# A transformer decoder's second feed-forward: inputs turned one tile ahead, second quantiser passes on GpSimd, the last norm's statistics in the loop, output stored by tiles

## The reference

```
def _act_quant(x):                       # per token
    scale = 127.0 / clip(max(abs(x), axis=-1), 1e-05)
    return clip(round(x * scale), -128, 127) / scale
def _weight_quant(w):                    # ternary, one scale for the whole matrix
    scale = 1.0 / clip(mean(abs(w)), 1e-05)
    return clip(round(w * scale), -1, 1) / scale
def _bitlinear(x, w):
    return einsum('bsd,fd->bsf', _act_quant(x), _weight_quant(w))
h = silu(_bitlinear(x, W1))              # W1: 2048 x 512
x = layernorm(x + _bitlinear(h, W2))     # W2: 512 x 2048, layernorm over the 512 features
```

## Time and profile before

| | |
|---|---|
| median of 3 runs | 3617.8 us (3613.61, 3617.80, 3622.76) |
| profiled execution, own time | 3619.58 us |
| profiled execution, span from first to last instruction | 3617.7 us |
| mean granted TensorE clock | 0.948 of full speed |
| busy share of the span: PE, DVE, ACT, POOL | 87%, 71%, 59%, 41% |
| HBM traffic | 110.75 MB read, 4.54 MB written |

### The profile page before, as it was taken

One profiled execution on the slowest core, in us unless ns is written; L12 is line 12 of the kernel. 1 busy time (PEld: TensorE's weight loads), 2 busy tenths in 40 slices (PEclk: granted clock), 3 DMA queues, 4 the chain that ended last, 5 costly groups with the idle time before them and its releaser, 6 DMA issues. The chain is left out here.

```text
span 3617.7 us, 82755 instructions
## 1 busy us (share of the span) xinstructions
PE 3130.8 (87%) x29792; PEld 2190.2 (61%) x29792; DVE 2583.4 (71%) x4821; ACT 2125.8 (59%) x5429; POOL 1492.7 (41%) x1849
## 2 busy tenths in 40 slices
PE   6999788268999999999999999999999999984185
PEld 4666565245666666666767667666676666763042
DVE  3444389865777777777777777777777777776876
ACT  4444400146777766777667776677766777763453
POOL 1111277114554545545445455455554554530000
PEclk9999899678999999999999999999999999996698
DMA  4000011001111011010110101101011010001201
GB/s 186 13 13 1 8 44 41 18 25 46 31 25 31 23 39 32 25 31 19 42 32 23 32 19 42 32 19 37 19 42 32 19 37 19 32 18 47 93 1 47
DMA packets 43231, 120.72 MB, mean 33 GB/s; under 512 B 5825, under 2 KB 10049, under 8 KB 39489
## 3 DMA queue, kind: packets, MB, share of 16 engines
q1 hardware_dynamic: 42816, 115.30, 10.2%
HBM read 110.75 MB, written 4.54 MB: 32 GB/s over the span
## 5 line engine op out<-in xcount | busy, mean ns | idle before, releaser
L2000 DVE TENSOR_TENSOR delta_Pb<-delta_bank,delta_lev 128x512 f16<-128x512 f32 x448 | 311.0, 694 | 230.9 <-PE delta_bank L2326 230.9
L1578 POOL TENSOR_SCALAR_AFFINE_SELECT delta_LA<-delta_LA 128x512 f32<-128x512 f32 x128 | 81.6, 637 | 857.3 <-DVE delta_LA L2021 848.1
L1992 DVE SCALAR_TENSOR_TENSOR delta_F<-delta_bank,delta_cw,delta_F 128x510 f32<-128x510 f32 (+1 forms) x512 | 380.8, 744 | 67.6 <-ACT delta_far L1811 57.5
L2300 PE MATMUL delta_bank<-delta_xh,delta_qkvh 128*128 128x512 f16 x1024 | 391.4, 382 | 4.5 <-DVE delta_qkvl L1960 3.0
L2300 PE MATMUL delta_bank<-delta_xl,delta_qkvh 128*128 128x512 f16 x1024 | 391.4, 382 | 0.0
L2300 PE MATMUL delta_bank<-delta_xh,delta_qkvl 128*128 128x512 f16 x1024 | 390.1, 381 | 0.0
L1598 POOL TENSOR_TENSOR delta_F<-delta_F,delta_far 128x506 f32<-128x506 f32 x256 | 283.6, 1108 | 255.6 <-DVE delta_F L1992 255.6
L1805 ACT ACTIVATE delta_F<-delta_bank,delta_cw 128x512 f32<-128x512 f32 x256 | 178.9, 699 | 280.9 <-PE delta_bank L2300 279.6
L2009 DVE CAST delta_XT<-delta_bank 128x512 f16<-128x512 f32 x448 | 309.4, 691 | 44.4 <-PE delta_bank L2349 44.3
L1770 ACT ACTIVATE delta_Xi<-delta_bank 128x512 f16<-128x512 f32 x320 | 190.1, 594 | 180.4 <-PE delta_bank L2345 180.4
L2285 PE MATMUL delta_bank<-delta_zh,delta_xh 128*128 128x256 f16 x1024 | 279.4, 273 | 0.6 <-ACT delta_gz L1833 0.6
(11 more groups left out here) (350 smaller groups left out, 9247.1 us busy)
## 6 DMA issues: line engine op xcount, KB each, us to landing
delta_Gb<-g_rows SPq DMA_DIRECT2D x66, 512.0 KB, 5.4
delta_st_qkv<-in_Wqkv SPq DMA_DIRECT2D x17, 1024.0 KB, 8.4
conv_T<-filters SPq DMA_DIRECT2D x32, 256.0 KB, 3.1
delta_st_zo<-in_Wz SPq DMA_DIRECT2D x16, 512.0 KB, 8.9
delta_st_zo<-in_Wout SPq DMA_DIRECT2D x16, 512.0 KB, 6.2
ffn_ahead_W<-in_W SPq DMA_DIRECT2D x2, 4096.0 KB, 17.6
conv_ahead_C<-in_ctx_rev SPq DMA_DIRECT2D x1, 6144.0 KB, 27.7
attn_xt<-in_xT SPq DMA_DIRECT2D x8, 512.0 KB, 4.6
```

Source lines behind the costliest of these rows:

```text
L1992: ve.scalar_tensor_tensor(dst, src, cw_tap(i, 3 - lag), dst, ALU.mult, ALU.add)\
L2000: ve.tensor_tensor(left(Pb[:, lvl, :, :], lvl), comp(bank[5], lvl), bc(lev[:, lvl, :].rearrange("p (n s) -> p n s", s=1 << lvl), 1, 8), AL ...
L2300: ins = te.matmul(bk[:, :], ww[:, QKV[job], kc, :], xx[:, kc, tok:tok + 512], start=(m == 0), stop=(m == 11))
```

## The change

Five things:

1. **Input turned one tile ahead.** PE, ACT and DVE do their step for x(t+1) in iteration t: PE turns it behind up(t), ACT copies it behind Silu(t), DVE quantises it ahead of quantise_h(t-1). Tile 0 is done ahead of the loop.
2. **Second quantiser passes on POOL.** The subtraction and clipping into xq and hq (before: L1176, L1189) are issued on POOL, in the order x(0), x(1), h(0), x(2), h(1), and so on. DVE no longer waits for its own first pass; PE waits for POOL's signals.
3. **Statistics in the loop.** `moments` makes each tile's mean and variance on DVE behind its residual add (in the iteration after it, and for the last tile behind the loop), into a tile that outlives the stage.
4. **Last norm.** `last_norm_stage` has no statistics of its own. It scales five tiles on ACT, five on POOL and six on DVE.
5. **Output stored tile by tile.** SP issues 16 DMAs of 256 KB in the same stage, each when its tile is scaled, in the order of the three engines' first tiles, second tiles, and so on. The separate store stage with its barrier is gone.

```diff
--- before.py
+++ after.py
@@ -1022,7 +1022,7 @@
                 last.then_inc(tr.sem, 1)
 
 
-def ffn1_stage(nc, X, consts, ahead):
+def ffn1_stage(nc, X, consts, ahead, mv):
 
     with ExitStack() as ctx:
         pt = Parts(nc, "ffn1", ctx)
@@ -1042,11 +1042,12 @@
         xf, xq = sb("xf", [P, 2, D]), sb("xq", [P, 2, D], BF16)
         xqT = sb("xqT", [P, 2, KC, P], BF16)
         h = sb("h", [P, 2, FF])
+        st = sb("st", [P, 2, 6])
         hq = sb("hq", [P, 2, FF], BF16)
         hqT = sb("hqT", [P, 2, FC, P], BF16)
         g = {n: counter(n, c) for n, c in dict(
-            ib=1, mg=1, ps=1, pd=1, wsum=1, tot=1, wsc=2, w1=4, w2=4, w3=4, mx=1, inv=3, x1=2, xt=1, xc=1, m1=4, sl=4,
-            hx=1, hs=3, hq=2, ht=4, hc=4, m2=1, add=1).items()}
+            ib=1, mg=1, ps=1, pd=1, wsum=1, tot=1, wsc=2, w1=4, w2=4, w3=4, mx=1, inv=3, x1=1, x2=1, xt=1, xc=1, m1=4, sl=4, st=1, mo=1,
+            hx=1, hs=3, h1=1, hq=1, ht=4, hc=4, m2=1, add=1).items()}
         block = ctx.enter_context(nc.Block())
 
 
@@ -1064,6 +1065,26 @@
                 gp.partition_all_reduce(sc[:, 4 * m + 1:4 * m + 2], sc[:, 4 * m:4 * m + 1], P,
                                         bass.bass_isa.ReduceOp.add).then_inc(g["tot"].sem, 1)
 
+            def rounded_x(t):
+                pool.wait_ge(g["x1"].sem, g["x1"].at(1, t))
+                if t >= 2:
+                    pool.wait_ge(g["xt"].sem, g["xt"].at(1, t - 2))
+                gp.tensor_scalar(xq[:, t % 2, :], xf[:, t % 2, :], MAGIC, 127.0, ALU.subtract, ALU.min)\
+                    .then_inc(g["x2"].sem, 1)
+
+            def rounded_h(t):
+                pool.wait_ge(g["h1"].sem, g["h1"].at(1, t))
+                if t >= 2:
+                    pool.wait_ge(g["ht"].sem, g["ht"].at(4, t - 2))
+                gp.tensor_scalar(hq[:, t % 2, :], h[:, t % 2, :], MAGIC, 127.0, ALU.subtract, ALU.min)\
+                    .then_inc(g["hq"].sem, 1)
+
+            rounded_x(0)
+            for t in range(NT):
+                if t + 1 < NT:
+                    rounded_x(t + 1)
+                rounded_h(t)
+
         @block.scalar
         def _(act):
             s_ = nc.scalar
@@ -1094,7 +1115,7 @@
                 for n in range(NB):
                     act.wait_ge(g["m1"].sem, g["m1"].at(n + 1, t))
                     if t >= 2 and n == 0:
-                        act.wait_ge(g["hq"].sem, g["hq"].at(2, t - 2))
+                        act.wait_ge(g["hq"].sem, g["hq"].at(1, t - 2))
                     s_.activation(h[:, t % 2, n * 512:(n + 1) * 512], bank[n][:, :], ACT.Silu,
                                   scale=tok[:, 0, t:t + 1]).then_inc(g["sl"].sem, 1)
 
@@ -1105,10 +1126,12 @@
                 s_.activation(xqT[:, t % 2, :, :].rearrange("p a b -> p (a b)"),
                               bank[4][:, 0:256].bitcast(BF16), ACT.Copy).then_inc(g["xc"].sem, 1)
 
+            xcopy(0)
             for t in range(NT + 1):
                 if t < NT:
-                    xcopy(t)
                     up(t)
+                if t + 1 < NT:
+                    xcopy(t + 1)
 
                 j = t - 1
                 if j >= 0:
@@ -1168,12 +1191,9 @@
                 dve.wait_ge(g["mx"].sem, g["mx"].at(1, t))
                 scales(0, t, None, 0, g["inv"])
                 xx = xf[:, t % 2, :]
-                ve.tensor_scalar(xx, X[:, t, :], inv[:, 0, t:t + 1], MAGIC, ALU.mult, ALU.add)\
-                    .then_inc(g["x1"].sem, 1)
-                dve.wait_ge(g["x1"].sem, g["x1"].at(1, t))
                 if t >= 2:
-                    dve.wait_ge(g["xt"].sem, g["xt"].at(1, t - 2))
-                ve.tensor_scalar(xq[:, t % 2, :], xx, MAGIC, 127.0, ALU.subtract, ALU.min).then_inc(g["x1"].sem, 1)
+                    dve.wait_ge(g["x2"].sem, g["x2"].at(1, t - 2))
+                ve.tensor_scalar(xx, X[:, t, :], inv[:, 0, t:t + 1], MAGIC, ALU.mult, ALU.add).then_inc(g["x1"].sem, 1)
 
             def quantise_h(t):
                 dve.wait_ge(g["sl"].sem, g["sl"].at(4, t))
@@ -1182,40 +1202,49 @@
                     .then_inc(g["hx"].sem, 1)
                 dve.wait_ge(g["hx"].sem, g["hx"].at(1, t))
                 scales(1, t, None, 1, g["hs"])
-                ve.tensor_scalar(hh, hh, inv[:, 1, t:t + 1], MAGIC, ALU.mult, ALU.add).then_inc(g["hq"].sem, 1)
-                dve.wait_ge(g["hq"].sem, g["hq"].at(1, t))
-                if t >= 2:
-                    dve.wait_ge(g["ht"].sem, g["ht"].at(4, t - 2))
-                ve.tensor_scalar(hq[:, t % 2, :], hh, MAGIC, 127.0, ALU.subtract, ALU.min).then_inc(g["hq"].sem, 1)
-
+                ve.tensor_scalar(hh, hh, inv[:, 1, t:t + 1], MAGIC, ALU.mult, ALU.add).then_inc(g["h1"].sem, 1)
+
+            def moments(t):
+                dve.wait_ge(g["add"].sem, g["add"].at(1, t))
+                ve.bn_stats(st[:, t % 2, :], X[:, t, :]).then_inc(g["st"].sem, 1)
+                dve.wait_ge(g["st"].sem, g["st"].at(1, t))
+                ve.bn_aggr(mv[:, t, :], st[:, t % 2, :]).then_inc(g["mo"].sem, 1)
+
+            quantise_x(0)
             for t in range(NT + 2):
-                if t < NT:
-                    quantise_x(t)
                 if t == 0:
                     weight_scale(1)
                     clipped(1)
+                if t + 1 < NT:
+                    quantise_x(t + 1)
                 if 0 <= t - 1 < NT:
                     quantise_h(t - 1)
                 j = t - 2
+                if j >= 1:
+                    moments(j - 1)
                 if j >= 0:
                     dve.wait_ge(g["m2"].sem, g["m2"].at(1, j))
                     ve.scalar_tensor_tensor(X[:, j, :], bank[7][:, :], tok[:, 1, j:j + 1], X[:, j, :], ALU.mult,
                                             ALU.add).then_inc(g["add"].sem, 1)
+            moments(NT - 1)
 
         @block.tensor
         def _(pe):
             te = nc.tensor
             pe.wait_ge(g["ib"].sem, g["ib"].at(1))
+
+            def turned_x(t):
+                pe.wait_ge(g["x2"].sem, g["x2"].at(1, t))
+                if t >= 1:
+                    pe.wait_ge(g["xc"].sem, g["xc"].at(1, t - 1))
+                for kc in range(KC):
+                    last = te.transpose(bank[4][:, kc * 64:(kc + 1) * 64].bitcast(BF16),
+                                        xq[:, t % 2, kc * P:(kc + 1) * P], ib[:, :])
+                last.then_inc(g["xt"].sem, 1)
+
+            turned_x(0)
             pe.wait_ge(g["w3"].sem, g["w3"].at(4))
             for t in range(NT + 2):
-                if t < NT:
-                    pe.wait_ge(g["x1"].sem, g["x1"].at(2, t))
-                    if t >= 1:
-                        pe.wait_ge(g["xc"].sem, g["xc"].at(1, t - 1))
-                    for kc in range(KC):
-                        last = te.transpose(bank[4][:, kc * 64:(kc + 1) * 64].bitcast(BF16),
-                                            xq[:, t % 2, kc * P:(kc + 1) * P], ib[:, :])
-                    last.then_inc(g["xt"].sem, 1)
                 if t < NT:
                     pe.wait_ge(g["xc"].sem, g["xc"].at(1, t))
                     for n in range(NB):
@@ -1225,9 +1254,11 @@
                             last = te.matmul(bank[n][:, :], xqT[:, t % 2, kc, :], w1q[:, kc, n * 512:(n + 1) * 512],
                                              start=(kc == 0), stop=(kc == KC - 1))
                         last.then_inc(g["m1"].sem, 1)
+                if t + 1 < NT:
+                    turned_x(t + 1)
                 j = t - 1
                 if 0 <= j < NT:
-                    pe.wait_ge(g["hq"].sem, g["hq"].at(2, j))
+                    pe.wait_ge(g["hq"].sem, g["hq"].at(1, j))
                     for n in range(4):
                         if n >= 2:
                             pe.wait_ge(g["hc"].sem, g["hc"].at(n - 1, j))
@@ -2529,15 +2560,63 @@
             turns(nc, ENG.PE, turn)
 
 
-def store_stage(nc, X, out):
+THIRDS = (range(0, 5), range(5, 10), range(10, NT))
+
+
+def last_norm_stage(nc, X, mv, out):
+
     with ExitStack() as ctx:
-        stored = Parts(nc, "store", ctx).counter("done", 0, 16)
+        pt = Parts(nc, "last", ctx)
+        var, rs, t, nb = (pt.sb(n, [P, NT]) for n in ("var", "rs", "t", "nb"))
+        variance, tab, newton, shift = (pt.counter(n) for n in ("var", "tab", "newton", "shift"))
+        by_act, by_pool, by_dve = (pt.counter(n) for n in ("by_act", "by_pool", "by_dve"))
+        stored = pt.counter("stored", 0, 16)
         block = ctx.enter_context(nc.Block())
 
         @block.sync
         def _(sp):
-            sp.dma_start(out.rearrange("b (h p) d -> p (b h) d", p=P), X[:, :, :]).then_inc(stored.sem, 16)
-            sp.wait_ge(stored.sem, stored.at(1))
+            for n in range(6):
+                for tiles, done in zip(THIRDS, (by_act, by_pool, by_dve)):
+                    if n < len(tiles):
+                        sp.wait_ge(done.sem, done.at(n + 1))
+                        sp.dma_start(out[:, tiles[n], :], X[:, tiles[n], :]).then_inc(stored.sem, 16)
```

(44 more changed lines are left out.)

## The result

The changed kernel is slower: 3647.45 us at the median (3642.7 to 3652.05, 4 runs) against 3620.09 for the kernel before (3613.61 to 3622.76, 4 runs), a ratio of 1.0078 [1.0056, 1.0101]. The forecast was 3599, faster. What happened is rival 3: POOL is so slow at these passes that its chain bounds the loop.

What follows compares the result with a forecast made beforehand. PE was taken to bound the feed-forward loop, with holes, and the end to be serial. The terms +0.9 - 7.15 + 0.85 + 0.87 - 9.65 - 4.9 sum to -19.1 us, giving 3599 us, chance 0.62; range 3592 to 3608.

Steps and rivals of the forecast that it cites:

- rival 3: Feed-forward loop: POOL so slow that its chain bounds the loop and more than eats the end's gain; 3633 us, chance 0.04.
- Period, 7.2 + S/2 from S = 4.8: Feed-forward loop: with S = H + Xp, POOL's two passes, its two-tile chain sets the period per tile from S = 4.8 us.
- 9.60 with POOL hidden: Steady feed-forward loop: POOL's passes are hidden and the period per tile is 9.60 us, 0.55 less than before.
- The slipped copies: ACT's queue: the input copy ahead of the four hidden copies moves the first from 4.25 to 4.78 us; without slipping, period 9.07.
- Start of the loop, +0.9: Tile 2's input waits behind hidden tile 0 on POOL, so its up-projection starts at 3438.0 instead of 3437.07, costing 0.9 us.
- PE's clock: Granted clock at the 1.2 GHz level in tile 2, behind the longer wait at the start, was named as a wrong sign.
- Ahead of the loop, 0: From the feed-forward stage's start to the first up-projection: a change of 0 us.
- Last tile, +0.85: End of the loop: POOL's 2.0 us plus 0.05 hand-over replaces DVE's 1.23, making the last tile 0.85 us later.
- The statistics' +0.87: After the last residual add: the last tile's statistics, 0.68 + 0.15 and a hand-over, cost 0.87 us.
- DVE and POOL "mostly miss each other": Feed-forward loop: DVE and POOL passes sharing a port lock mostly do not overlap, so the forecast loses nothing.
- rival 2: POOL at a two-input pace, H = 3.75 and Xp = 1.1: 3606 us with DVE's input pass caught, upper bound 3618; chance 0.14.
- Last norm, -9.65 and store, -4.9: Kernel's end: statistics leaving the last norm gain 9.65 us; the first store issued earlier, by tiles, gains 4.9 us.

Runs made afterwards that it cites:

- kernel 7: kernel 4 with 44 unused matmuls in odd tiles ahead of PE's wait for POOL; 1.0065 against the kernel before, 3639.29 us.
- run 1: The changed kernel with both second quantiser passes back on DVE; 0.9944 against the kernel before, 3595.16 us.
- run 3: The changed kernel with only the input's second pass on POOL, the hidden tile's back on DVE; 0.9928 against the kernel before, 3589.23 us.
- run 9: The changed kernel with POOL's two tensor-scalars replaced by casts, the clip at 127 left out; 0.9944 against the kernel before, 3596.37 us.
- run 10: The changed kernel with only the input's pass on POOL, hidden copies ahead of the input copy, last norm on ACT and DVE; 0.9903 against the kernel before, 3581.09 us.
- run 6: The kernel before with only the new end: statistics in the loop, last norm on three engines, stores by tile; 0.9953, 3599.88 us.
- run 8: The kernel before plus a POOL memset and one-column tensor-scalar beside its store; 0.998, 3608.84 us.
- kernel 4: The changed kernel with DVE's first input pass on ACT, both second passes still on POOL; 1.0079 against the kernel before, 3644.68 us.
- run 2: The changed kernel with only the hidden tile's second pass on POOL, the input's back on DVE; 1.0043 against the kernel before, 3632.89 us.
- run 5: The kernel before with only the two second quantiser passes on POOL, old order and old end; 1.0081, 3645.75 us.

## Why the prediction was wrong

**The step that failed** is the size of two terms: "I take H = 2.0 us for the hidden tile and Xp = 0.65 us for the input tile, and keep 1.9 and 5.3 as bounds of H." H is 7.08 and Xp 1.97. The price was read from the row with the same kinds of operands, the cast, and the upper bound from a row with two tensors. Neither holds the new operation's arithmetic, and the bound was no bound: the tensor-scalar costs more than both. The prediction knew that POOL's pace was the open question, and that the sum is zero near H = 5.2 and +11 near 3 ns a column; it gave this 0.04, because "No row of POOL is that slow". A row that is not there was taken for evidence against.

Step by step:

- *Period, 7.2 + S/2 from S = 4.8:* right in its mechanism. With S = 9.05 it gives 11.73; kernel 7, which takes the clock away, measures 12.19, of which 0.43 is POOL's slowed input pass.
- *9.60 with POOL hidden:* right, 9.54 (runs 1, 3, 9). The slipped copies were the reason that it was not less: run 10 puts them first and gets 9.06, the prediction's 9.07.
- *Start of the loop, +0.9:* the same two prices make it +7.3, measured +9.2. 1.8 of the rest is PE's clock behind the wait of 9.23 us (7.58 - 5.76). The prediction had named this clock as a sign of being wrong, but had no term for it. In runs 1 and 9, without the slow passes, it was +1.3 and +1.8; but runs 6 and 8, whose loop is the old one, have 12.9 and 12.8 there too, so a term of 0.9 is below what these executions resolve.
- *Ahead of the loop, 0:* wrong. The first input's pass was moved to POOL, and the prediction did not follow it past the all-reduce in POOL's queue, nor knew of the idle time behind it: +2.4.
- *Last tile, +0.85:* +5.95 by H, and 1.95 on top because PE, after 6.48 us idle, did a part of the tile at the 1.2 GHz level. The statistics' +0.87 was right.
- *DVE and POOL "mostly miss each other":* the text said that with a slower POOL they meet, and they do (4.11 us for L1196). It had 3 us for that in rival 2; kernel 7 shows some 5 for its kind of meeting. The changed kernel's 13 periods exceed the formula by 8.9 us, and its own trace divides them. Followed back from tile 15 by its waits for POOL, the path is six chains over two tiles and one plain tile of 9.54 us. In three of the chains POOL gets the hidden tile late, at 10.48, 10.28 and 9.49 us in place of 8.56, because DVE's stretched input pass holds up the maximum: 4.6 us in all. In four the link from the turning to L1254 is slow, 8.45, 7.44, 6.87 and 6.55 us in place of 5.76, with the granted clock at 0.50 in it: 6.3. The plain tile takes 2.2 off, and small hand-overs are the rest.
- *PE's clock:* named only for tile 2, with no term in the sum. It cost 1.8 us there, 6.3 in the 13 periods and 2.0 in the last tile, the largest single part of what the right prices leave open. Filling the wait in kernel 7 gave 8.5 us of the stretch against kernel 4.
- *Last norm, -9.65 and store, -4.9:* right to a hundredth, as far as the first store. That "the three engines make one in 0.8 to 1.2 us" was wrong by the same price: a tile takes POOL 2.1 us. In the changed kernel this costs little (+0.7), since POOL has its idle time behind the all-reduce already behind it. Where POOL has not run since the all-reduce, or ran only casts, it costs 5 us (runs 1, 6, 9).

Of the 16 us by which the measured stretch exceeds the formula with the right prices, the table gives the places: 8.9 in the periods, 2.4 and 1.9 ahead of them, 2.0 in the last tile. By cause, some 10 are PE's clock and 4.6 DVE's late maximum.

## What to carry to other kernels

Before work is moved to an engine that the trace does not show at it, measure that one operation alone: here no row of another operation bounded it, not even one with more operands; and when the sum turns on this price, say what the sum is where the price is several times worse and give that a real chance. Then follow the moved instruction through the new engine's queue, with what that engine does just ahead of it. And a wait on PE can cost more than its length where it is followed by matmuls: look at the granted clock behind it.

## What the hardware showed

- POOL's tensor-scalar with two operations: 1.09, 1.92, 3.62 and 7.08 us for 256, 512, 1,024 and 2,048 columns, some 3.3 ns for each further column, and at 2,048 the same for the three pairs of f32 and bf16 that were run; the cast 1.89 for 2,048.
- Between the all-reduce and a tensor-scalar, in either order, POOL is idle for 5.9 to 7.7 us; where it had waited long for a semaphore its tensor-scalar came 4.3 to 4.6 us late (runs 1 and 6). The effect outlasts an execution: with a tensor-scalar of one column at the end of the kernel the first affine select of a repeated execution comes 7.2 us earlier.
- The granted clock fell to 0.50, the 1.2 GHz level, in or behind PE's waits of 2.80 (run 2), 4.40, 6.48 and 9.23 (changed kernel) and 5.45 us (run 4). The length of the wait alone does not say when: it also fell behind waits of 1.94 (run 5) and 1.31 us (changed kernel, at 3541), and not behind one of 1.76 (at 3554). With the wait of 5.45 filled with matmuls it stayed at 1.00 (run 7).
- A DVE operation with two SBUF tensors beside POOL's tensor-scalar took 4.48 us and still ended first; a tensor-scalar ended with POOL's, within 0.3 us.
- Sixteen stores of 256 KB, issued as the tiles come, end as soon as one store of 4 MB: 13.2 us from the first issue, against 13.3.
